# First attention stage: where the negated maxima are rounded, how masks and near products are cut, and the order of PE's work

## The reference

```python
sim = einsum('bhid,bhjd->bhij', q, k)            # 64 (batch, head) pairs, 1024 x 1024
sim = sim + transpose(rel_emb[bucket(i - j)]) * SCALE
sim = sim + where(j > i, -inf, 0)                # causal
attn = softmax(sim, axis=-1)
out = einsum('bhij,bhjd->bhid', attn, v)         # then @ Wo.T + bo, added to x
```

## Time and profile before

| | us |
|---|---|
| median of 3 runs | 1818.81 (1814.5 to 1819.84) |
| profiled execution, its own time | 1816.17 |
| its span, first to last instruction | 1814.4 |
| busy in the span: PE | 1637.8 (90%) |
| DVE | 1508.2 (83%) |
| ACT | 1255.7 (69%) |
| POOL | 781.9 (43%) |

### The profile page before, as it was taken

How to read it: one execution, slowest core, us unless ns; L and a number is a source line. 1 busy time by engine, 2 the same in 40 slices (tenths; PEclk the granted TensorE clock), 3 DMA queues, 4 the chain that set the end, 5 groups by cost and what they waited for, 6 DMA issues and landing times. The chain is left out here.

```text
span 1814.4 us, 48183 instructions
## 1 busy us (share of the span) xinstructions
PE 1637.8 (90%) x19082; PEld 1046.8 (58%) x19082; DVE 1508.2 (83%) x2238; ACT 1255.7 (69%) x2481; POOL 781.9 (43%) x1501
## 2 busy tenths in 40 slices
PE   5599999999877999999999649999999999999945
PEld 3376666676665878776777414444444444444434
DVE  7599999999676999986555769999999999999553
ACT  6388888888743445444333628898898989898944
POOL 5488888888744010000000324444444444444444
PEclk9699999999956999999999868999999999999977
DMA  7522232323264667761000351111121121112121
GB/s 247 199 83 85 88 94 86 96 85 97 71 116 68 95 90 95 91 90 37 1 1 0 137 185 46 58 52 59 54 70 53 57 69 54 58 54 71 42 57 35
DMA packets 119908, 141.86 MB, mean 78 GB/s; under 512 B 22221, under 2 KB 80778, under 8 KB 119690
## 3 DMA queue, kind: packets, MB, share of 16 engines
q1 hardware_dynamic: 119258, 138.79, 30.5%
q10 hardware_dynamic: 432, 0.07, 0.0%
HBM read 92.70 MB, written 44.98 MB: 76 GB/s over the span
## 5 line engine op out<-in xcount | busy, mean ns | idle before, releaser
L887 DVE TENSOR_REDUCE heads_mx<-heads_psM 128x1 f32<-128x1024 f32 x512 | 602.5, 1220 | 48.0 <-PE heads_psM L978 32.1
L958 ACT ACTIVATE heads_probs<-heads_psS 128x512 f32<-128x512 f32 x1024 | 545.9, 600 | 77.4 <-PE heads_psS L1001 71.5
L927 POOL TENSOR_TENSOR heads_masked<-heads_probs,g_tri 128x128 f32<-128x128 f32 x512 | 233.2, 456 | 360.9 <-ACT heads_probs L958 360.7
L653 POOL TENSOR_TENSOR heads_probs<-heads_probs,one_ebias 128x256 f32<-128x256 f32 (+1 forms) x512 | 342.1, 694 | 76.4 <-ACT heads_probs L685 76.3
L614 DVE TENSOR_REDUCE heads_mx<-heads_psM 128x1 f32<-128x1024 f32 (+7 forms) x512 | 349.5, 750 | 23.6 <-PE heads_psM L696 22.5
L685 ACT ACTIVATE heads_probs<-heads_psS 128x512 f32<-128x512 f32 x576 | 316.2, 602 | 67.4 <-PE heads_psS L696 62.2
L978 PE MATMUL heads_psM<-three_kS,three_qS 48*128 48x512 bf16 x1024 | 230.2, 394 | 20.8 <-PEq L1960 11.9
L1001 PE MATMUL heads_psS<-three_qS,three_kS 50*128 50x512 bf16 x1024 | 237.6, 388 | 0.7 <-ACT heads_probs L958 0.3
L1509 ACT ACTIVATE trees_hid_hi<-trees_hid 128x512 fp32r<-128x512 f32 x192 | 121.7, 634 | 151.9 <-DVE trees_hid L1530 151.0
L1530 DVE SCALAR_TENSOR_TENSOR trees_hid<-trees_psH,g_b,trees_chosen 128x512 f32<-128x512 f32 x192 | 143.9, 750 | 31.4 <-DMA trees_chosen<-leaf_choice 14.4
L1026 PE MATMUL heads_psO<-heads_probs,heads_ones_only 128*32 128x128 f32 x1920 | 162.0, 284 | 0.0
(11 more groups left out here) (253 smaller groups left out, 3136.3 us busy)
## 6 DMA issues: line engine op xcount, KB each, us to landing
trees_chosen<-leaf_choice SPq DMA_DIRECT2D x96, 256.0 KB, 7.3
head_outputs<-g_small SPq DMA_DIRECT2D x128, 128.0 KB
one_qS<-q_parts SPq DMA_DIRECT2D x128, 96.0 KB
one_kS<-k_parts SPq DMA_DIRECT2D x128, 96.0 KB
three_qS<-q_parts SPq DMA_DIRECT2D x128, 96.0 KB
three_kS<-k_parts SPq DMA_DIRECT2D x128, 96.0 KB
q_parts<-g_w SPq DMA_DIRECT2D x8, 768.0 KB, 4.5
k_parts<-g_w SPq DMA_DIRECT2D x8, 768.0 KB, 5.8
```

What stands on the lines that cost most here:

```text
L653: pool.tensor_tensor(pr[:, a:a + w], pr[:, a:a + w], bass.AP(eb.tensor, eb.offset + NEAR - 1, [list(eb.ap[0]), [-1, w]]), ALU.mult).then_i ...
L887: dve.tensor_reduce(mx[:, n % 2, k:k + 1], psM[k % 2][:, :], AXX, ALU.max, negate=True).then_inc(max_taken, 1)
L927: pool.tensor_tensor(masked[n % 2][:, kb, :], probs[n % 2][:, kb, kb * P:(kb + 1) * P], g["tri"][:, 0:P], ALU.mult).then_inc(near_done, 1)
L958: act.activation(probs[n % 2][:, kb, h * CH:(h + 1) * CH], ring.bank(i)[:, :], ACT.Exp).then_inc(slot_taken, 1)
```

## The change

- **Maxima.** The reductions of `attend_causal` negate. DVE's two operations at L624 and L626 go; POOL does them as a cast and a subtraction (`minus_maxima`), for head `n + 2` before its last product of head `n`, and for heads 0 and 1 before its first.
- **Near products.** Eight become five (`NEARS`): (0, 1), (2, 3) and (5, 4) are one product of 2 x 256 columns each. `values` part 0 waits for four of the five, part 1 for all. `VALUES` is cut anew: 9, 10 and 7 products instead of 13, 6 and 7.
- **Masks.** `mask` covers the 128 columns of a diagonal block by two products of 64 columns, with two different weight tables, instead of two products of 128 whose sums add up. The tables are made by 14 POOL steps in the opening, one waiting for the other, and copied by one DMA.
- **Maxima's products.** In `maxima` the products of the two banks alternate, and the masks come behind them all, first halves, then second halves.
- **Order on PE.** Each `maxima` step moves two places ahead, `rows(n + 1)` moves in front of `values(n - 1, 0)`.

The core of the diff (the constants' tables and names are left out in part):

```diff
-                pool.memset(g["masks"][:, :, :, :], 0.0).then_inc(made, 1)
+                pool.memset(g["masks"][:, :, :], 0.0).then_inc(made, 1)
...
-                for table, op, fill, sign in ((0, ALU.not_equal, 1.0, -1), (1, ALU.is_ge, NEG, -1), (2, ALU.is_ge, NEG, 1)):
-                    t = g["masks"][:, 0, table, :]
-                    pool.affine_select(out=t, in_=t, compare_op=op, fill=fill, base=0, pattern=[[sign, P]], channel_multiplier=-sign).then_inc(made, 1)
...
+
+                def choose(table, at, width, op, fill, base, step, down):
+
+                    t = g["masks"][0:HALF, table, at:at + width]
+                    pool.affine_select(out=t, in_=t, compare_op=op, fill=fill, base=base, pattern=[[step, width]],
+                                       channel_multiplier=down).then_inc(masked, 1)
+                    masks_made[0] += 1
+                    pool.wait_ge(masked, masks_made[0])
...
+                masks_made = [0]
+                for table, last in ((0, HALF - 1), (1, 0)):
+                    choose(table, 0, P, ALU.not_equal, 1.0, 0, -1, 1)
+                    choose(table, P, P, ALU.not_equal, 1.0, HALF, -1, 1)
+                    alone = (last - 1, -1) if last else (-1, 1)
+                    choose(table, 0, P, ALU.is_ge, 0.0, alone[0], 0, alone[1])
+                    choose(table, P, P, ALU.is_ge, 0.0, alone[0], 0, alone[1])
+                    if table == 0:
+                        choose(0, P, P, ALU.is_ge, 1.0, P * last - HALF, 1, -P)
+                        choose(0, 2 * P, HALF, ALU.is_ge, NEG, 0, -1, 1)
+                    else:
+                        choose(1, 0, P, ALU.is_ge, 1.0, HALF - 1, -1, P)
+                        choose(1, 2 * P, HALF, ALU.is_ge, NEG, 0, 1, -1)
+                    choose(table, 2 * P, HALF, ALU.is_ge, NEG, alone[0], 0, alone[1])
...
-    NEAR_ORDER = [0, 1, 7, 2, 6, 3, 5, 4]
-    NEAR_AFTER = [0, 2, 3, 4, 5, 6, 7, 8]
-    VALUES = [[(0, 0), (1, 0), (2, 0), (3, 0), (0, 1), (1, 1), (2, 1), (3, 1), (0, 2), (1, 2), (2, 3), (3, 4), (0, 3)],
-              [(0, 4), (1, 3), (2, 2), (3, 2), (0, 5), (1, 4)],
-              [(0, 6), (1, 5), (2, 4), (3, 3), (0, 7), (1, 6), (2, 5)]]
-
-    ENDS = VALUES[2][-4:]
+    NEARS = [((0, 1), 2), ((7,), 3), ((6,), 5), ((2, 3), 6), ((5, 4), 8)]
+    NEAR_FIRST = 4
+    VALUES = [[(0, 0), (1, 0), (2, 0), (3, 0), (0, 1), (1, 1), (2, 1), (3, 1), (0, 2)],
+              [(1, 2), (2, 2), (3, 2), (0, 3), (1, 3), (2, 3), (3, 4), (0, 4), (1, 4), (0, 5)],
+              [(2, 4), (3, 3), (0, 6), (1, 5), (2, 5), (0, 7), (1, 6)]]
+
+    ENDS = [(3, 3), (2, 5), (0, 7), (1, 6)]
 
...
-                        last = dve.tensor_reduce(mx[:, p, qb:qb + 1], psM[(n * NM + i) % 2][:, at:at + w], AXX, ALU.max)
+                        last = dve.tensor_reduce(mx[:, p, qb:qb + 1], psM[(n * NM + i) % 2][:, at:at + w], AXX, ALU.max, negate=True)
...
                     last.then_inc(max_taken, 1)
-                dve.wait_ge(max_taken, (n + 1) * NM)
-                dve.wait_ge(block_taken, (n + 1) * (TPB - NM))
-                if n >= 2:
-
-                    dve.wait_ge(slot_done, ring.rows(n - 2) + 1)
-                dve.tensor_scalar(nm[:, p, 0, :], mx[:, p, :], -1.0, None, ALU.mult).then_inc(nm_hi, 1)
-                dve.wait_ge(nm_hi, n + 1)
-                dve.scalar_tensor_tensor(nm[:, p, 1, :], mx[:, p, :], -1.0, nm[:, p, 0, :], ALU.mult, ALU.subtract).then_inc(nm_ready, 1)
+
...
+            def minus_maxima(n):
+
+                p = n % 2
+                pool.wait_ge(max_taken, (n + 1) * NM)
+                pool.wait_ge(block_taken, (n + 1) * (TPB - NM))
+                if n >= 2:
+                    pool.wait_ge(slot_done, ring.rows(n - 2) + 1)
+                pool.tensor_copy(nm[:, p, 0, :], mx[:, p, :]).then_inc(nm_hi, 1)
+                pool.wait_ge(nm_hi, n + 1)
+                pool.tensor_tensor(nm[:, p, 1, :], mx[:, p, :], nm[:, p, 0, :], ALU.subtract).then_inc(nm_ready, 1)
+
+            def weight(n, blocks):
+
+                pr, eb, w = probs[n % 2][:, :], g["ebias"][:, n % HEADS, :], near_width(blocks[0])
+                a = place(blocks[0], blocks[0])
+                step = place(blocks[-1], blocks[-1]) - a
+                at = bass.AP(pr.tensor, a, [list(pr.ap[0]), [step, len(blocks)], [1, w]])
+                by = bass.AP(eb.tensor, eb.offset + NEAR - 1, [list(eb.ap[0]), [0, len(blocks)], [-1, w]])
+                pool.tensor_tensor(at, at, by, ALU.mult).then_inc(near_done, 1)
+
             stage_v(0)
+            minus_maxima(0)
+            minus_maxima(1)
             for n in range(NG):
-                pr = probs[n % 2]
-                for kb, unit in zip(NEAR_ORDER, NEAR_AFTER):
+                for blocks, unit in NEARS:
                     pool.wait_ge(slot_taken, ring.index(n, unit) + 1)
-                    a, w = place(kb, kb), near_width(kb)
-                    eb = g["ebias"][:, n % HEADS, :]
-                    pool.tensor_tensor(pr[:, a:a + w], pr[:, a:a + w], bass.AP(eb.tensor, eb.offset + NEAR - 1, [list(eb.ap[0]), [-1, w]]),
-                                       ALU.mult).then_inc(near_done, 1)
+                    weight(n, blocks)
+                    if unit == NEARS[-2][1] and n + 2 < NG:
+                        minus_maxima(n + 2)
                 if n + 1 < NG:
...
-            def mask(out, r, table):
-
-                for s in range(2):
-                    done = pe.matmul(out, g["masks"][r:r + HALF, s, 0, :], g["masks"][r:r + HALF, s, table, :], start=False, stop=s == 1)
+            def mask(out, r, table, stop=True):
+
+                m2 = g["masks"][r:r + HALF, table, :]
+                for half in range(2):
+                    done = pe.matmul(out[:, half * HALF:(half + 1) * HALF], m2[:, half * P:(half + 1) * P], m2[:, 2 * P:2 * P + HALF],
+                                     start=False, stop=stop and half == 1)
                 return done
...
-                at = 0
+                runs, ends, at = ([], []), [], 0
                 for qb in MAXIMA[i]:
                     w = (qb + 1) * P
                     for bank in range(2):
                         a, z = max(at, bank * CH), min(at + w, (bank + 1) * CH)
-                        if a >= z:
-                            continue
-                        r, ends = HALF * bank, z == at + w
-                        last = pe.matmul(ps[:, a:z], qS[u][r:r + PROWS, qb * P:(qb + 1) * P], kS[u][r:r + PROWS, a - at:z - at], start=True, stop=not ends)
-                        if ends:
-                            last = mask(ps[:, z - P:z], r, 1)
+                        if a < z:
+                            runs[bank].append((qb, a, z, a - at))
                     at += w
+                    ends.append(at)
+                for j in range(max(len(of) for of in runs)):
+                    for bank in range(2):
+                        if j < len(runs[bank]):
+                            qb, a, z, first = runs[bank][j]
+                            r = HALF * bank
+                            pe.matmul(ps[:, a:z], qS[u][r:r + PROWS, qb * P:(qb + 1) * P], kS[u][r:r + PROWS, first:first + z - a],
+                                      start=j == 0, stop=j + 1 == len(runs[bank]) and (bank + 1) * CH not in [-(-e // CH) * CH for e in ends])
+                for half in range(2):
+                    for z in ends:
+                        r, at = HALF * ((z - 1) // CH), z - P + half * HALF
+                        m2, later = g["masks"][r:r + HALF, 0, :], [e for e in ends if z < e <= -(-z // CH) * CH]
+                        last = pe.matmul(ps[:, at:at + HALF], m2[:, half * P:(half + 1) * P], m2[:, 2 * P:2 * P + HALF], start=False,
+                                         stop=half == 1 and not later)
                 last.then_inc(maxima_done, 1)
...
-                        last = mask(ps[:, at:at + P], r, 2)
+                        last = mask(ps[:, at:at + P], r, 1)
...
-                    pe.wait_ge(near_done, (n + 1) * TPB)
+                    pe.wait_ge(near_done, n * len(NEARS) + NEAR_FIRST)
...
+                if part == 1:
+                    pe.wait_ge(near_done, (n + 1) * len(NEARS))
...
                 maxima(1, i)
+            maxima(2, 0)
+            maxima(2, 1)
             for n in range(NG):
                 scores(n, 0)
                 scores(n, 1)
-                maxima(n + 2, 0)
-                maxima(n + 2, 1)
+                maxima(n + 2, 2)
+                maxima(n + 2, 3)
                 scores(n, 2)
                 scores(n, 3)
+                rows(n + 1)
                 values(n - 1, 0)
-                rows(n + 1)
                 scores(n, 4)
-                maxima(n + 2, 2)
+                maxima(n + 2, 4)
                 scores(n, 5)
                 scores(n, 6)
-                maxima(n + 2, 3)
+                maxima(n + 3, 0)
                 values(n - 1, 1)
                 scores(n, 7)
                 scores(n, 8)
```

(16 more changed lines are left out.)

## The result

The changed kernel takes 1810.37 us (median of 5 runs, 1808.77 to 1814.31), beside it the kernel before 1817.74 (1814.5 to 1819.84). The ratio is 0.9966, with a 95% interval of 0.9952 to 0.9980, which is 3.6 to 8.7 us. The medians differ by 7.4 us, where 9.7 were forecast. The profiled execution of the changed kernel took 1814.3 us (its span is 1812.6); it is the longest of its five.

What follows compares the result with a forecast made beforehand. DVE was taken as the bound at 6.28 us per head, row DMAs second, PE third. Steps -11.2 and start +1.5 gave -9.7: 1816.2 to 1806.5, plus 2.6 for the median, 1809.0 us; range 1774 to 1826.

Steps and rivals of the forecast that it cites:

- The bound: In `attend_causal`, DVE closes undisturbed steps at 6.28 us per head; the row DMAs come second, PE third.
- The sum of the step: PE's path from one head's `scores(n, 0)` to the next: 2.93 + 1.18 + 2.04 = 6.15 us, against 6.28.
- ACT's start behind `scores(n, 0)`: ACT begins unit 0 of a head 0.48 us after PE starts its scores, down from 0.53.
- PE's reaction: 0.05 us allowed between ACT finishing unit 1 and PE starting `rows`, which then starts at 1.89 us.
- `rows` to `values`: On PE, `rows` takes 0.05 us before `values` part 0 follows.
- Landings: Shift-row copy ends at 2.98 us, not 3.26, so steps set by the row DMAs' arrival shorten by 0.28.
- The term of the stage's steps: The 60 head-to-head steps of `attend_causal` together lose 11.2 us off 387.6.
- the prediction's own rule: Each head's step is the larger of 6.15 us and its time before less 0.28.
- Start: The first `scores(0, 0)` waits for DVE to finish head 1's maxima: 1.5 us charged (0 to 3).
- The wait doesn't bite: Rival: `rows` finds its bank free of ACT, PE's step is 5.65 us, total 1783; chance 0.17.
- the landings eat it: Rival: row DMAs arrive 0.3 us later behind the head's loads, undoing the 0.28; total 1816; chance 0.21.
- The weight load sets the mask's step: Rival: PE's 64-column masks step by 0.055 to 0.095 us, not 0.028; total 1825 to 1851; chance 0.15.

Runs made afterwards that it cites:

- `masks_pool`: The changed kernel with both moves in PE's order undone (shift rows and maxima back in their old places): 1802.3 us, ratio 0.9911 to the kernel before.

## Why the prediction held, point by point

**The bound.** Right that DVE has no hole in the undisturbed step, and that relieving it doesn't help unless PE shortens too. Wrong is the order: the prediction called PE third, but the kernel with GpSimd's part alone shows it at 6.29, level with DVE's 6.28. So DVE didn't close the step alone.

**The sum of the step**, in the order of the prediction, from the rows of after:
- ACT's start behind `scores(n, 0)`: 0.48 expected, 254.69 - 254.21 = 0.48. Unit 1 comes 0.75 later (0.76 expected) and takes 0.60. Right.
- PE's reaction, 0.05 allowed: `rows` starts 1.98 behind `scores(n, 0)`, not 1.89. **This term failed by 0.09**: the wait for the bank sits in an instruction of its own before the weight load.
- `rows` to `values`, 0.05: measured 0.13. **It failed by 0.08**: the wait instruction of `values` used to be worked off while PE streamed the scores; behind a bare wait it is not.
- `values` part 0 and the change of mode, 0.89 + 0.10: 257.32 - 256.32 = 1.00. `scores 4` to part 1, 1.18: 1.16. Part 1 to the next head, 2.04: 2.04. Right, and with them the mask's step of 0.03 (two records of 0.189 span 0.22).

So 6.31 and not 6.15. With the waits written in the other order the same products give 6.12: `rows` starts 0.08 sooner behind `scores(n, 0)` and `values` 0.12 sooner behind `rows`. So both missed terms are the handling of waits.

**Landings.** The copy now ends at 257.13, 2.92 behind `scores(n, 0)` (2.98 expected); with the longer step the margin is 3.39, not 3.17. Longer steps are 11 instead of 25 and hold 5.9 us instead of 10.8. In sum the 60 steps went from 387.1 to 383.5 us: 3.6 less, where 11.2 were forecast. **The term of the stage's steps was sized three times too large**, in these two executions. The two missed waits explain it: the prediction's own rule, each step the larger of 6.31 (and not 6.15) and its time before less 0.28, gives 383.6, which is 4.0 off its 387.6 and not 11.2. The rule held, and its term for the undisturbed step did not.

The two profiled executions differ by 1.9 us (1816.2 and 1814.3), the medians by 7.4. What follows `scores(63, 0)`, where only the stage's end was changed, took 1327.1 us before, 1328.3 after and 1323.5 to 1329.4 over the other profiled executions, so a single pair can't settle 4 us. That 1809.0 lies 1.4 us from 1810.4, with its largest term three times too large, is luck as far as these traces show; where the rest of the 7.4 us comes from stays open.

**The rest.** Start: `scores(0, 0)` at 78.49 instead of 77.79, 0.7 where I charged 1.5; but against the kernel without the early maxima (76.06) they cost 2.4; the shorter masks give most of the other 1.7 back, since with them alone it comes at 76.28. POOL: cast to product 0.43 (0.41 expected), 5.4 us per head. Opening, POOL's timeline:

```profile
3.03 5.34 POOL L320 TENSOR_SCALAR_AFFINE_SELECT g_masks<-g_masks 64x128 bf16<-64x128 bf16 x14
...
16.42 1.27 POOL L348 TENSOR_TENSOR g_x<-g_x,g_bo 128x512 f32<-128x512 f32 x1 [2.57 <-DMA g_bo<-in_L_attn_bo]
```

The 14 steps take 5.3 us, and 2.6 us of waiting for the DMA are left: it cost nothing.

**The rivals.** "The wait doesn't bite" is out: it bites in each of 61 heads. Its step of 5.65 was about right for PE's path (5.75 with the rows put back), but it couldn't have given 1783 us: that kernel takes 1806.5, though its copy ends as early behind `scores(n, 0)`. There "the landings eat it" is the true mechanism. In the steps shown, SP has issued the last load of k 1.9 us before the row DMAs in the changed kernel (255.26 to 257.15) and 1.3 us before them in the kernel `masks_pool` (255.46 to 256.78), and the median landing there comes 3.17 and no longer 3.01 us behind the copy. SP's queue in `masks_pool`:

```profile
254.05 1.41 SPq L511 DMA_DIRECT2D one_kS<-k_parts  x2
255.51 0.58 SPq L515 DMA_DIRECT2D head_outputs<-g_small  x1
256.78 1.37 SPq L526 DMA_DIRECT2D one_qS<-heads_mrow  x2
```

"The weight load sets the mask's step" is out, at 0.03.

## What to carry to other kernels

Before moving an instruction up, look at which wait it then meets bare, and at how many semaphores it waits for: one that is always met in time belongs in front, and the late one on the instruction itself (here the wait written first ended up there). When several engines and a DMA close a step within a few tenths of a microsecond of each other, single parts of a change are worth little and together much; what decides is the second bound, here a small transfer behind large ones on the same queue, and the cure was more distance, not more speed.

## What the runs showed that was not expected

- A wait instruction that PE works off unseen in a stream costs about 0.1 us when it stands behind a bare wait: 0.08 us in front of `rows`, 0.12 in front of `values`. The two made 0.19 us per head (6.31 to 6.12).
- The later of the two 4 KB row DMAs never landed sooner than 2.44 us behind the copy that fed it in the 60 steps of any kernel, even with next to nothing else on the queue, and 0.5 us (median before) to 2.9 us (longest of all) later with 384 KB of loads per head around it. The Trainium skill, DMA: Bandwidth & Descriptors, section "Anatomy of one DMA — SWDGE (gpsimd) path", gives about 2.0 us of fixed cost for another issuing path; the trace is of that order, with 0.7 us of it for issuing the first of the two DMAs.
